# First row tile normalized alone, W1 loaded in halves, and the first product in two parts, in a two-layer graph kernel on one core

## What is computed

```
h = max(layernorm(x), 0)
x = x + GAT2(elu(GAT1(h)))     # GAT1: 768 -> 4 heads x 512, GAT2: 2048 -> 768, attention softmax over incoming edges
h = max(layernorm(x), 0)
x = x + GCN2(relu(GCN1(h)))    # 768 -> 768 twice, degrees normalized
```

## Time and profile before

| | |
|---|---|
| median of 3 runs | 1159.08 us (1156.29 to 1159.99) |
| the profiled execution | 1161.38 us |
| its span | 1159.5 us |
| TensorE (PE) busy in the span | 1113.2 us, 96% |
| Vector (DVE) busy | 850.5 us, 73% |
| ScalarE (ACT) busy | 512.3 us, 44% |
| GpSimd (POOL) busy | 27.5 us, 2% |
| mean granted clock of TensorE | 0.991 of full speed |

### The profile page before, as it was taken

The page is one execution under the profiler, slowest core; times in us unless marked ns, Lnnn a source line. Parts: engine busy times, 40 slices in busy tenths (PEclk is TensorE's granted clock), DMA queues, the critical chain, the costliest instruction groups (busy, mean ns, idle before and its releaser), DMA issues.

```text
span 1159.5 us, 17646 instructions
## 1 busy us (share of the span) xinstructions
PE 1113.2 (96%) x7126; PEld 1044.8 (90%) x7126; DVE 850.5 (73%) x1431; ACT 512.3 (44%) x1056; POOL 27.5 (2%) x40
## 2 busy tenths in 40 slices
PE   5999999988999999999999999989999999999998
PEld 4878886788999999999999999979998999899998
DVE  7998898888879888898879777689777533341263
ACT  4232322276446655575446665255537521431110
POOL 4200000020000000000000000000000000000000
PEclk9999999998999999999999999989999999999999
DMA  6134232021003100201003000031012200100321
GB/s 234 53 120 114 71 128 73 1 64 55 1 29 100 34 23 14 90 25 55 1 28 101 29 1 1 1 123 52 28 56 79 82 1 2 28 14 1 134 83 52
DMA packets 29347, 63.17 MB, mean 54 GB/s; under 512 B 3684, under 2 KB 6344, under 8 KB 29264
## 3 DMA queue, kind: packets, MB, share of 16 engines
q1 hardware_dynamic: 29072, 61.68, 16.5%
q10 hardware_dynamic: 192, 0.32, 0.1%
HBM read 46.45 MB, written 15.54 MB: 53 GB/s over the span
## 4 chain that ended last, share of the span: by engine, by line
PE 68%; DVE 7%; DMA 1%; ACT 1%; issue 1%; DVEq 0%; ACTq 0%
PE banks L1535 20%; PE banks L1565 14%; PE banks L2080 9%; PE banks L2203 6%; PE banks L2196 5%; PE banks L2145 5%; PE banks L2119 4%; PE banks L1517 2%; DVE top L1058 1%; ACT e L250 1%; DMA w_st<-in_L_gnn_W 1%; PE banks L235 1%; DVE pf L269 1%; DVE e L267 1%; DVE w_lo L1101 0%
## 5 line engine op out<-in xcount | busy, mean ns | idle before, releaser
L1535 PE MATMUL banks<-hs,ring_hi 128*128 128x258 f32 (+1 forms) x1600 | 303.0, 290 | 4.3 <-DVE z L1122 4.3
L1535 PEld LDWEIGHTS banks<-hs,ring_hi 128*128 128x128 f32 (+1 forms) x1600 | 250.8, 190 | 6.2 <-DVE z L1122 4.5
L1535 PE MATMUL banks<-hs,ring_lo 128*128 128x258 f32 (+1 forms) x800 | 228.3, 285 | 0.0
L250 ACT ACTIVATE e<-banks,al 128x256 f32<-128x256 f32 (+1 forms) x450 | 180.5, 494 | 8.4 <-PE banks L235 8.4
L258 ACT ACTIVATE ring_hi<-pf 128x512 fp32r<-128x512 f32 (+1 forms) x125 | 81.7, 653 | 173.0 <-DVE pf L269 169.9
L1535 PEld LDWEIGHTS banks<-hs,ring_lo 128*128 128x128 f32 (+1 forms) x800 | 152.0, 190 | 0.0
L1565 PE MATMUL banks<-w_hi,oT_hi 128*128 128x386 f32 (+3 forms) x320 | 109.4, 342 | 3.4 <-DVE shiftT L1211 3.2
L1565 PE MATMUL banks<-w_lo,oT_hi 128*128 128x386 f32 (+3 forms) x320 | 108.7, 340 | 0.0
L1565 PE MATMUL banks<-w_hi,oT_lo 128*128 128x386 f32 (+3 forms) x320 | 108.2, 338 | 0.0
L267 DVE TENSOR_TENSOR e<-e 128x512 f32<-128x512 f32 (+1 forms) x125 | 84.6, 677 | 24.9 <-ACT e L250 24.6
L1409 PE MATMUL banks<-w_hi,xT_hi 128*128 128x512 f32 x240 | 96.7, 403 | 1.3 <-DVE xT_lo L879 0.8
(11 more groups left out here) (273 smaller groups left out, 2129.0 us busy)
## 6 DMA issues: line engine op xcount, KB each, us to landing
w_st<-in_L_gnn_W SPq DMA_DIRECT2D x26, 384.0 KB, 3.2
h_scratch<-stage SPq DMA_DIRECT2D x30, 256.0 KB, 2.0
hs<-h_scratch SPq DMA_DIRECT2D x30, 256.0 KB, 2.9
w_st<-in_L_gnn_W SPq DMA_DIRECT2D x4, 1536.0 KB, 7.4
gw_st<-in_L_gnn_W SPq DMA_DIRECT2D x12, 384.0 KB, 4.0
xr<-in_x SPq DMA_DIRECT2D x9, 384.0 KB, 10.2
rows<-in_x SPq DMA_DIRECT2D x9, 384.0 KB, 3.9
x_scratch<-rows SPq DMA_DIRECT2D x9, 384.0 KB
```

The lines of the kernel that those rows point to most:

```text
L250: last = nc.scalar.activation(self.e[:, local % 2, a, i, 0:n], self.p_shift[:, a, 0:n], ACT.Exp, bias=scores[a][:, g * G + i:g * G + i + 1])
L1535: last = nc.tensor.matmul(p_a[0:m, dt, half, 0:HH], wt.ring[a][:, s // G, s % G, dt * P:dt * P + m], hs[:, s, b, half * HH:(half + 1) * HH ...
```

## The change

- The sets of `PARTS` become tile 0 alone, tiles 1 and 2, tiles 3 to 5, tiles 6 to 9.
- W1 of the first head is loaded in two DMAs of three blocks (FRONT = 3): the first behind row tile 0, the second behind row tile 1. The first half has a semaphore of its own, `w_front`.
- ACT: the root of set 0 ahead of the floats of the edges; the root of set 1 behind the high parts of weights 0 to 2, of row tile 0 and of weight 3; the root of set 2 behind the first edge copies.
- Vector: a new order. The factors of tiles 1 and 2 come ahead of the low part of tile 0, the statistics of tile 3 ahead of the low part of tile 1, the factors of tiles 3 to 5 behind the statistics of 4 and 5, and `dest_spans` moves behind the third low part.
- TensorE: the edges are transposed first, then row tile 0; the transposes of row tile 1 stand in the middle of the first product, between its third and fourth block.
- The semaphore for picked chunks is merged into the one for turned edges.

```diff
@@ -152,11 +152,12 @@
         a_in = keep.enter_context(nc.semaphore("a_in"))
+        w_front = keep.enter_context(nc.semaphore("w_front"))
         tile_in = [keep.enter_context(nc.semaphore(f"tile_in{t}")) for t in range(T)]

-        def load_weights(sp, i):
+        def load_weights(sp, i, ks=slice(0, KD)):
             h = ORDER[i]
-            sp.dma_start(mem.w_st[:, :, :], W1.rearrange("(k p) n -> p k n", p=P)[:, :, h * HID:(h + 1) * HID]).then_inc(w_in, 16)
+            sp.dma_start(mem.w_st[:, ks, :], W1.rearrange("(k p) n -> p k n", p=P)[:, ks, h * HID:(h + 1) * HID]).then_inc(w_front if ks.start == 0 and ks.stop < KD else w_in, 16)

@@ -164,7 +165,7 @@
         with ExitStack() as st:
-            first_layer(nc, st, mem, x, src, dst, W2, b1, as2, ad2, h_scratch, w_in, a_in, load_weights, load_vectors, tile_in,
+            first_layer(nc, st, mem, x, src, dst, W2, b1, as2, ad2, h_scratch, w_in, w_front, a_in, load_weights, load_vectors, tile_in,
                         (x, b2, G1, c1, G2, c2, x2_scratch, out))
@@ -290,7 +291,8 @@

-PARTS = [(0, 3), (3, 6), (6, T)]
+PARTS = [(0, 1), (1, 3), (3, 6), (6, T)]
+FRONT = KD // 2
 FIRST_COUNT = 9
...
@@ -387,9 +389,8 @@
     edges_out_done = sem("edges_out_done")
-    et_done = sem("edges_and_spans_turned")
+    et_done = sem("edges_turned")
     spread_ready = sem("spread_ready")
-    picked = sem("picked")
     red_ready = sem("red_ready")
@@ -509,8 +510,8 @@
                 sp.dma_start(xr[0:rows_of(t), t, :], x[t * P:t * P + rows_of(t), :]).then_inc(tile_in[t], 16)
-                if t == 2:
-                    load_weights(sp, 0)
+                if t < 2:
+                    load_weights(sp, 0, slice(t * FRONT, (t + 1) * FRONT))
             load_vectors(sp, 0)
@@ -616,7 +617,10 @@
             def weight_hi(i, ks=range(KD)):
-                act.wait_ge(w_in, 16 * (i + 1))
+                if i == 0 and ks[0] < FRONT:
+                    act.wait_ge(w_front, 16)
+                else:
+                    act.wait_ge(w_in, 16 * (i + 1))
                 for k in ks:
@@ -647,19 +651,21 @@

-            def edges_out(sources, dests, n, done):
-                act.wait_ge(done, 1)
+            def edges_out(sources, dests, n, turn):
+                act.wait_ge(et_done, turn)
                 nc.scalar.activation(sources, p_e[:, 0, 0:n], ACT.Copy).then_inc(edges_out_done, 1)
...

+            deviations(0)
             edges_float()
-            deviations(0)
-            weight_hi(0, range(0, 3))
+            weight_hi(0, range(0, FRONT))
             turned_hi(0)
-            weight_hi(0, range(3, KD))
+            weight_hi(0, range(FRONT, FRONT + 1))
+            deviations(1)
+            weight_hi(0, range(FRONT + 1, KD))
             turned_hi(1)
-            edges_out(e_src[:, :], e_dst[:, :], NCH, et_done)
-            deviations(1)
+            edges_out(e_src[:, :], e_dst[:, :], NCH, 1)
+            deviations(2)
             for n in range(FIRST):
@@ -673,9 +679,9 @@
                 if n == 3:
-                    deviations(2)
+                    deviations(3)
                 if n == 6:
-                    edges_out(s_i[:, :], d_f[:, :], NW * FIX, picked)
+                    edges_out(s_i[:, :], d_f[:, :], NW * FIX, 3)
                 for g in groups_after(n):
@@ -975,22 +981,26 @@
             nc.vector.memset(xr[96:P, T - 1, :], 0.0).then_inc(pad_zero, 1)
-            row_parts(range(0, 3))
+            row_parts(range(0, 1))
             factors(0)
+            row_parts(range(1, 2))
+            weight_lo(0, range(0, 2))
+            row_parts(range(2, 3))
+            factors(1)
+            turned_lo(0)
+            weight_lo(0, range(2, KD))
+            row_parts(range(3, 4))
+            turned_lo(1)
+            row_parts(range(4, 6))
+            factors(2)
+            turned_lo(2)
             dest_spans()
-            weight_lo(0, range(0, 3))
-            turned_lo(0)
-            weight_lo(0, range(3, KD))
-            turned_lo(1)
-            row_parts(range(3, 6))
-            factors(1)
-            turned_lo(2)
             chunk_windows()
...
             row_parts(range(8, T))
-            factors(2)
+            factors(3)
             turned_lo(5)
@@ -1382,7 +1392,7 @@
                                                 start=j == 0, stop=j == EJ - 1)
-                last.then_inc(picked, 1)
+                last.then_inc(et_done, 1)

@@ -1392,15 +1402,15 @@

-            def tile(n):
+            def tile(n, ks=range(KD)):
                 i, t = n // T, n % T
...
                         pe.wait_ge(hlo_done, n - 1 - FIRST)
-                u = 0
-                for k in range(KD):
+                u = 3 * ks[0]
+                for k in ks:
                     if t == 0:
@@ -1411,7 +1421,8 @@
                         last.then_inc(w_free, 1)
-                last.then_inc(h_ready, 1)
+                if ks[-1] == KD - 1:
+                    last.then_inc(h_ready, 1)

@@ -1431,11 +1442,15 @@
             pe.wait_ge(made, 12)
-            for t in range(2):
-                turn_rows(t)
             transpose_edges()
+            turn_rows(0)
             for n in range(FIRST):
-                tile(n)
+                if n == 0:
+                    tile(0, range(0, FRONT))
+                    turn_rows(1)
+                    tile(0, range(FRONT, KD))
+                else:
+                    tile(n)
                 if n + 2 < T:
...
                 if n in beside:
```

More of the change, by code:

```diff
@@ L298, in mask_slot, with first_layer @@
     return (t + NDT) % T
-def first_layer(nc, st, mem, x, src, dst, W2, b1, as2, ad2, h_scratch, w_in, a_in, load_weights, load_vectors, tile_in, later):
+def first_layer(nc, st, mem, x, src, dst, W2, b1, as2, ad2, h_scratch, w_in, w_front, a_in, load_weights, load_vectors, tile_in, later):
     pb, sem = makers(nc, st)
```

## The result

The changed kernel took **1162.95 us** (median of 20 runs, 1159.83 to 1166.99), the kernel before 1159.95 beside it (20 runs, 1156.29 to 1164.48): ratio **1.0026, 95% interval 1.0015 to 1.0038**, some 3.0 us slower. The interval is clear of 1, and the size is under the 0.3% that was set as the bound. The forecast was 1162.5, no change or a little slower.

The account below looks back on a forecast made before the run. Vector's time to the fourth low part was taken as the bound: 2.1 us from its new order plus 1.3 us from TensorE's low clock made +3.4 us, the median going from 1159.08 to 1162.5 us, range 1159.4 to 1165.4.

Parts of the forecast that it names:

- The landings: Input transfers in the new order: row tile 1 lands at 8.9 us, row tile 2 at about 11.90.
- The start: First product on TensorE at 15.8 instead of 16.30, held by row tile 0's low part on Vector; gain 0.5 us.
- Vector to the third low part: Vector's new order at high clock: third low part starts at 24.91, 0.86 us later than before.
- The clock: TensorE idles 4.7 us ahead of the first product, whose nine matmuls then run at low clock; cost 1.3 us.
- The sign that I named for it: The profile would show a granted clock of 0.50 at the first product, near 15.8 us.
- The edge bounds and the windows: Edge bounds of 1.24 us stand ahead of unchanged 5.74 us windows on Vector; fourth low part 2.1 us late.
- my sum with the clock: Start of the fourth low part on Vector: 32.76 at high clock, plus 1.3 us for the low clock.
- Nothing behind absorbs it: Time lost up to the fourth low part stays lost, as later waits shift with Vector or TensorE; total +3.4 us.
- second low stretch: Rival: a 2.05 us wait ahead of the fourth product lowers TensorE's clock again, costing 1.6 us; 1164.1 us, chance 0.23.
- clock didn't stay high: Refers to the rival that TensorE's clock is high at the first product, 15.8 us; +2.1 us, 1161.2 us, chance 0.20.
- The change does what it says: Rival: the first product starts with half of W1, near 12 us; a gain, faster given 0.03 in all.
- Collisions go: Rival: Vector's low weight (0.63) and chunk windows (0.45) no longer collide with GpSimd; +1.0 us, 1160.1 us, chance 0.08.

Follow-up runs that it names:

- g1: The changed kernel plus 20 transposes of the identity on TensorE between row tile 0's transposes and the first product; ratio 0.9992.
- f4: a1 plus 17 transposes of the identity on TensorE ahead of the edge transposes and 34 behind row tile 0; 1160.01 us, ratio 0.9999.
- a1: The changed kernel with the edge bounds moved on Vector from behind the third low part to behind row tile 0's factors; 1163.1 us, ratio 1.0021.
- b1: The kernel before with only the edge bounds moved on Vector to behind the third low part; ratio 1.0010.
- f3: b1 plus 46 transposes of the identity on TensorE ahead of its first work; 1157.90 us, ratio 0.9982.
- h1: f1 with the fourth low part on Vector moved into the middle of the chunk windows; 1157.95 us, ratio 0.9975.
- h3: f1 with the edits of both h1 and h2; 1157.68 us, ratio 0.9969.
- h2: f1 with two casts of the picked chunks moved from Vector to ACT; 1158.20 us, ratio 0.9980.
- a3: The changed kernel with row tile 0's low part on Vector ahead of the statistics and factors of row tiles 1 and 2; ratio 1.0017.
- f1: The kernel before plus 46 transposes of the identity on TensorE ahead of its first work; 1158.18 us, ratio 0.9986.
- f2: The changed kernel plus 17 transposes of the identity on TensorE ahead of the edge transposes and 34 behind row tile 0; 1159.99 us, ratio 0.9994.
- a2: The changed kernel plus 24 matmuls of the identity on TensorE between row tile 0's transposes and the first product; 1161.88 us, ratio 1.0024.

## Why the prediction was right, and where its terms were off

**The landings: right.** Row tile 2 was expected at about 11.9 and tile 1 at 8.9; Vector took them up at 11.84 and 8.82.

**The start: right.** 15.8 was expected, 15.74 measured: the early transposes (9.79 instead of 12.62) bought nothing, as the low part of tile 0 stands behind the factors of tiles 1 and 2 (14.64). Once the first tiles were in, ACT and GpSimd, costed at nothing, let nobody wait for them by more than 0.32 us (TensorE at 27.41, for GpSimd), but for the high part of row tile 1, which was late by TensorE's clock.

**Vector to the third low part: right.** With the fast pace I had the low part of tile 1 at 19.92 and that of tile 2 at 24.91; g1, moved to the same first statistics, has 19.99 and 24.98. The collision of a low weight with GpSimd stayed, as costed: four took 3.27, against 2.51 and 1.88 for three beside GpSimd and after it.

**The clock: right, in size and in kind.** 1.3 us was taken from a row 245 us away; g1 gives 1.23, and the pair f4 and a1 1.45. The sign that I named for it was wrong: I expected a granted clock of 0.50 in that stretch, and the column shows 1.00. The Trainium skill, "TensorE: Matmul & The Clock Gate", Wait — 56ns, not 53.3ns?, puts the start-to-start time of a cold array at the columns over 1.2 GHz, 426.7 ns for 512; the trace has 16.31, 16.73, 17.16, 17.59, which agrees. By the same page's section What's actually happening the point of the rise isn't tied to the kernel's start and differs between runs; the runs agree (fast by 16.30 in the kernel before, 18.87 after the change, 21.3 in b1).

**The edge bounds and the windows: the step that failed.** In "Now the edge bounds: 12.67 less 0.21 of idle less 11.22 = 1.24 us, ... right ahead of the windows of the chunks, 24.92 to 30.66 = 5.74" the windows are mis-sized by 0.92 us. The edge bounds did cost their 1.27 (27.05 to 28.32). But the windows took 4.82: 1.27 us later they lie beside GpSimd's row tiles 3 to 5 for 1.7 us and not for 3.2. a1, f3 and f4 show it from both sides: edge bounds taken out, 5.73 and 5.74; put in, 5.00; and b1, clear of GpSimd, has 4.35. The duration of a group that runs beside GpSimd belongs to its place and mustn't be carried along. I had this as a rival of its own and gave collisions 0.08, for the low weight and the windows together; the low weight's stayed, and of the windows' 1.39 (5.74 less 4.35) 0.92 went, twice the 0.45 that the rival had. The Trainium skill, "SBUF — State Buffer", Who interferes with whom, has Vector operations with two inputs in SBUF contend with GpSimd's reads, and reductions never. The windows' products, 1.72 beside GpSimd and 1.04 behind it, are of the first kind; in b1, where the edge bounds (reductions) and a low part lay beside GpSimd, its three row tiles took 2.91, three times the 0.98 of a single one in the changed kernel, and the bounds their usual 0.66 each. That agrees.

With that the fourth low part lands where it was measured: 33.19 counted from 5.20, where my sum with the clock has 34.06. TensorE's wait ahead of product 4 is 1.18 and not 2.05, the same 0.87, and the profile's loss is 2.56 at the last row tile and 2.77 at the last hot wait, not 3.4. The median's +3.0 (+1.7 to +4.4 by the interval) lies with both, so the total can't tell a loss of 2.6 from one of 3.4, and its nearness to the forecast is no proof of the sum.

**"Nothing behind absorbs it": right, with its reason open.** The lateness stays to 220 us. I gave it to Vector's time to the fourth low part, and the wait of 1.18 there is indeed ended by Vector. But half of the loss (1.23) came in as TensorE's low pace, which reached Vector through the high part of row tile 1, and behind 32 us h1 to h3 don't say which engine sets the pace. What the runs show is narrower: what delayed TensorE and Vector together ahead of 32 us was not made up, on whatever engine it arose, and Vector relieved by itself behind that was worth nothing in h2.

**The rivals.** No second low stretch came behind the wait ahead of product 4, which stayed 1.18. The clock didn't stay high. "The change does what it says" was built as a3, and even a first product at 13.19 gave nothing. "Collisions go" came in part, as said.

## What to carry to other kernels

Before work is brought forward, ask which engine the next wait ends on: here the early transposes ended on Vector's low part and the early first product on a low weight and on GpSimd, and a lead is worth something only if it outlasts the waits behind it. TensorE given a little work early and then left idle may still be at the lower clock when the real work comes; a fill of useless matmuls that ends before that work prices it in one run. And a group of two-input Vector operations that lies beside GpSimd has no fixed price: the same windows took from 4.35 to 5.74 us here, by where they began.

## What had not been expected of the hardware

- The profile's clock column showed 1.00 over a stretch in which 512 columns took 0.427 us (15.80 to 19.20), and likewise over the twelve transposes of the kernel before. Ahead of the first low stretch that is recorded, only the pace tells.
- The pace rose at different places in like executions: by 16.3 in the kernel before, at 21.3 in b1, whose TensorE has the same work in the same order up to there. Behind 1.98 of idle time the products of a3 ran slowly, as had the transposes ahead of it; behind 1.86 in g1, with 20 transposes more ahead, they ran fast. One trace each can't price a change of some 3 us that hangs on this.
- A fill from 4.2 us on raised the pace well before the first products in f1 (7 transposes in the us from 7.2, 11 in that from 8.2). In f2, with a pause of 1.40 us behind its first fill, the second still had 7 to the us up to 16.6; in f4, with a pause of 0.22, it had 10 in the us from 13.4 and 12 in the next.
- An fp32 matmul of the identity, 128 columns, costs about twice a transpose of the same size: 24 of them are 48 records in a2, 11 records to the us at the fast pace (15.0 to 16.0), where f4 has 12 transposes to the us (14.4 to 15.4).
- A low stretch that the clock column does show lay between 190 and 210 us in five of the fourteen traces (a1, a2, f1, g1, h3: 0.79 on average from 198 to 206, 1.00 in the others). The way from the last hot wait to the transposes of the greatest scores took 124.8 to 124.9 us in these five and 123.7 to 123.8 in the rest: 1.1 us. It is in g1 and not in the two main traces, one more reason to read the early landmarks and not the totals.
- Casts from int32 to uint16 of 125x490 took 1.0 us each on ACT (2.01 for two in h2), and hold Vector for some 0.45 (57.22 to 57.66 in f1).
